# Causal attention block on one core: the triangle of the diagonal steps added on TensorE instead of selected on GpSimd

## The reference

```
xm = layernorm(x, g1, be1) * (1 + sc_a) + sh_a
q, k, v = split(xm @ Wqkv)
scores = q @ k.T * 32**-0.5
scores = where(tril, scores, -inf)          # causal: key <= query
x = x + gt_a * ((softmax(scores) @ v) @ Wproj + bproj)
xm = layernorm(x, g2, be2) * (1 + sc_m) + sh_m
x = x + gt_m * (gelu(xm @ W1 + b1) @ W2 + b2)
```

## Time and profile before

| | |
|---|---|
| median of three runs | 2166.22 us (2165.55 to 2166.54) |
| profiled execution, span | 2163.8 us |
| TensorE busy | 2126.4 us, 98% |
| VectorE busy | 1290.6 us, 60% |
| GpSimd busy | 958.5 us, 44% |
| ScalarE busy | 930.1 us, 43% |
| attention's score matmuls, first and last start | 332.2 and 1356.8 us |

### The profile page before, as it was taken

How to read it: one execution, slowest core, us unless ns; L and a number is a source line. 1 busy time by engine, 2 the same in 40 slices (tenths; PEclk the granted TensorE clock), 3 DMA queues, 4 the chain that set the end, 5 groups by cost and what they waited for, 6 DMA issues and landing times.

```text
span 2163.8 us, 30729 instructions
## 1 busy us (share of the span) xinstructions
PE 2126.4 (98%) x11326; PEld 1428.5 (66%) x11326; DVE 1290.6 (60%) x2872; ACT 930.1 (43%) x1780; POOL 958.5 (44%) x383
## 2 busy tenths in 40 slices
PE   8999999999999999999999999999999999999999
PEld 7888885444544445454544544778888888888887
DVE  5878877777777777777777756784312312122122
ACT  2111115566566666666666566435322222222221
POOL 2001007989799797988979784770000000000000
PEclk9999999999999999999999999999999999999999
DMA  7448347234361523625244324694201011011010
GB/s 287 180 156 265 134 168 186 49 89 107 70 143 47 122 55 76 142 65 132 51 95 94 70 70 135 202 326 156 97 1 59 15 44 59 1 59 59 1 39 20
DMA packets 129310, 223.29 MB, mean 103 GB/s; under 512 B 8574, under 2 KB 26054, under 8 KB 128968
## 3 DMA queue, kind: packets, MB, share of 16 engines
q1 hardware_dynamic: 108568, 180.43, 30.6%
q10 hardware_dynamic: 20592, 40.90, 5.0%
HBM read 146.31 MB, written 74.98 MB: 102 GB/s over the span
## 4 chain that ended last, share of the span: by engine, by line
PE 78%; POOL 11%; DVE 5%; issue 3%; DMA 2%; ACT 1%; SPq 0%; POOLq 0%; DVEq 0%; ACTq 0%; PEldq 0%
PE m_hid L1973 16%; PE p_acc L1987 16%; PE acc L861 12%; POOL psum_k L1208 10%; PE st L1453 9%; PE mx L1433 9%; PE o_ps L1470 9%; PE r_ps L1477 2%; DVE part L1313 2%; PE r_ps L1491 1%; PE p_acc L1952 1%; PE misc L815 1%; PE acc L839 1%; PE tp L825 1%; ACT prob L1252 1%
## 5 line engine op out<-in xcount | busy, mean ns | idle before, releaser
L1252 ACT ACTIVATE prob<-st 128x512 f32<-128x512 f32 (+3 forms) x1280 | 609.1, 540 | 374.3 <-PE st L1453 353.5
L1208 POOL TENSOR_TENSOR psum_k<-psum_k,prob 128x2048 f32<-128x2048 f32 (+1 forms) x150 | 663.9, 4426 | 20.7 <-ACT prob L1252 5.8
L1313 DVE TENSOR_REDUCE part<-mx 128x1 f32<-128x512 f32 x707 | 457.9, 685 | 75.0 <-PE mx L1433 70.6
L1453 PE MATMUL st<-q_st,k_st 98*128 98x512 f32 (+3 forms) x1280 | 491.0, 395 | 4.0 <-PE r_ps L1477 1.4
L1433 PE MATMUL mx<-k_st,qx_st 96*128 96x512 f32 (+3 forms) x1196 | 442.8, 395 | 10.3 <-DVE part L1313 2.8
L1453 PEld LDWEIGHTS st<-q_st,k_st 98*128 98x128 f32 x1280 | 241.3, 189 | 267.2 <-ACT prob L1252 152.3
L1874 DVE TENSOR_TENSOR m_g_lo<-m_g,m_g_hi 128x512 fp32r<-128x512 f32 x128 | 88.6, 692 | 479.7 <-ACT m_g_hi L1791 479.5
L1433 PEld LDWEIGHTS mx<-k_st,qx_st 96*128 96x128 f32 x1196 | 223.5, 189 | 129.9 <-DVE part L1313 60.4
L1470 PE MATMUL o_ps<-prob,v_sb 128*32 128x512 f32 (+3 forms) x2560 | 297.4, 539 | 3.7 <-POOL prob L1191 3.7
L1309 DVE CUSTOM_DVE_ANT_0 unused<-mx,mask_row 128x512 bf16<-128x512 f32 (+2 forms) x489 | 228.9, 486 | 119.0 <-PE mx L1433 109.0
L1784 ACT ACTIVATE m_g<-m_hid,vcol 128x512 f32<-128x512 f32 x128 | 88.3, 690 | 471.5 <-PE m_hid L1973 471.4
(11 more groups left out here) (186 smaller groups left out, 2529.2 us busy)
## 6 DMA issues: line engine op xcount, KB each, us to landing
k_st<-qk_scratch SPq DMA_DIRECT2D x96, 256.0 KB, 8.0
qx_st<-qk_scratch SPq DMA_DIRECT2D x96, 256.0 KB, 5.0
q_st<-qk_scratch SPq DMA_DIRECT2D x96, 256.0 KB
qk_scratch<-st_hi ACTq DMA_DIRECT2D x16, 1024.0 KB, 4.2
qk_scratch<-st_lo ACTq DMA_DIRECT2D x16, 1024.0 KB, 6.9
xs<-in_x_dram SPq DMA_DIRECT2D x8, 1024.0 KB, 8.9
v_sb<-v_scratch SPq DMA_DIRECT2D x8, 1024.0 KB, 15.6
o_scratch<-o_sb SPq DMA_DIRECT2D x32, 256.0 KB, 2.3
```

Source lines behind the costliest of these rows:

```text
L1208: nc.gpsimd.tensor_tensor(dst, src, prob[:, s % BUF, :, m:], ALU.add).then_inc(pool_added, 1)
L1252: nc.scalar.activation(prob[:, s % BUF, h, m:], st[n % RING][:, m:], ACT.Exp, scale=SCALE).then_inc(exp_done, 1)
L1313: nc.vector.tensor_reduce(most, bank[:, 0:w], AX.X, ALU.max).then_inc(mx_free, 1)
L1453: nc.tensor.matmul(st[n % RING][:, m:], k_st[u][0:MROWS, h, kt * P:(kt + 1) * P], q_st[0:MROWS, pos % 2, h, m:], start=True, stop=True).th ...
```

## The change

The constants get two more members, a bf16 identity `ident_bf` and `mask_col`, a 128 x 128 bf16 tile that holds 0 where key <= query and -1e30 elsewhere (keys on partitions). For each head of a diagonal step TensorE issues a second matmul behind the score matmul, with the identity as weights and `mask_col` as moving operand, into the leftmost 128 columns of the same bank and in the same accumulation group. The score then holds -1e30 in the triangle, and its exponential is zero. `select` and all waits on `b_masked` go, from GpSimd and from TensorE. The counts of the constants' semaphore go from 5 to 9 and from 6 to 10. No item of the plan moves; the planner's prices are as they were.

```diff
@@ constants, GpSimd, start of phase_qkv
-            pool.wait_ge(c_ready, 3)
+            nc.gpsimd.memset(K.ident_bf[:, :], 0.0).then_inc(c_ready, 1)
+            nc.gpsimd.memset(K.mask_col[:, :], 0.0).then_inc(c_ready, 1)
+            pool.wait_ge(c_ready, 5)
...
+            nc.gpsimd.affine_select(out=K.ident_bf[:, :], in_=K.ident_bf[:, :], compare_op=ALU.not_equal, fill=1.0, base=0,
+                                    pattern=[[-1, P]], channel_multiplier=1).then_inc(c_ready, 1)
+            nc.gpsimd.affine_select(out=K.mask_col[:, :], in_=K.mask_col[:, :], compare_op=ALU.is_ge, fill=NEG,
+                                    base=0, pattern=[[1, P]], channel_multiplier=-1).then_inc(c_ready, 1)
@@ TensorE, start
-            pe.wait_ge(c_ready, 5)
+            pe.wait_ge(c_ready, 9)
@@ GpSimd, attention
-            def select(g, s):
-                n, m = L.selects.index(s), L.mid(s)
-                await_count(pool, held_pool, exp_done, exp_count(g, GH * (s + 1)))
-                tri = prob[:, s % BUF, :, m:m + P]
-                nc.gpsimd.affine_select(out=tri, in_=tri, compare_op=ALU.is_ge, fill=0.0, base=0,
-                                        pattern=[[0, GH], [1, P]], channel_multiplier=-1).then_inc(masked, 1)
@@ add, GpSimd
-                if L.diagonal(s):
-                    pool.wait_ge(masked, mask_count(g, L.selects.index(s) + 1))
@@ body, GpSimd
-                    if s in L.selects:
-                        select(g, s)
@@ scores, TensorE
-                    nc.tensor.matmul(st[n % RING][:, m:], k_st[u][0:MROWS, h, kt * P:(kt + 1) * P],
-                                     q_st[0:MROWS, pos % 2, h, m:], start=True, stop=True).then_inc(st_ready, 1)
+                    ins = nc.tensor.matmul(st[n % RING][:, m:], k_st[u][0:MROWS, h, kt * P:(kt + 1) * P],
+                                           q_st[0:MROWS, pos % 2, h, m:], start=True, stop=not L.diagonal(s))
+                    if L.diagonal(s):
+                        ins = nc.tensor.matmul(st[n % RING][:, m:m + P], K.ident_bf[:, :], K.mask_col[:, :], start=False, stop=True)
+                    ins.then_inc(st_ready, 1)
@@ product, TensorE
-                if L.diagonal(s):
-                    pe.wait_ge(masked, mask_count(g, L.selects.index(s) + 1))
```

More of the change, by code:

```diff
@@ L73, in __init__ @@
         self.ones = sb("ones", [P, P])
+        self.ident_bf = sb("ident_bf", [P, P], BF16)
+        self.mask_col = sb("mask_col", [P, P], BF16)
         self.vcol = sb("vcol", [P, V_ROWS])
@@ L207, in __init__ @@
         self.NA = self.sums[True].NA
-        self.selects = [s for s in range(self.NS) if self.diagonal(s)]
-        self.ND = len(self.selects)
         FROM = -3
@@ L969, in phase_attention @@
         exp_done = sem("b_exp_done")
-        masked = sem("b_masked")
         pv_done = sem("b_pv_done")
@@ L990, in phase_attention @@
         held_dve = sem("b_dve_wait_carrier")
-        held_pool = sem("b_pool_wait_carrier")
         def st_count(g, tiles):
@@ L1005, in add_count @@
             return L.NA * g + n + L.NA
-        def mask_count(g, n):
-            return L.ND * g + n
         def item_count(g, n):
@@ L1181, in key_ones @@
             def key_ones(h):
-                pool.wait_ge(masked, mask_count(0, sum(r <= ONES + h for r in L.selects)))
                 pool.wait_ge(pool_added, add_count(0, L.NA))
@@ L1549, in tensor @@
             pe.sem_inc(r_ready, 2)
-            pe.wait_ge(E.c_ready, 6)
+            pe.wait_ge(E.c_ready, 10)
             pe.wait_ge(E.mx_free, len(L.opening))
```

## The result

The changed kernel takes 2184.8 us (median of 4 runs, 2183.7 to 2185.9), the kernel before 2166.2 in the same session: ratio 1.0085, interval 1.0073 to 1.0097, so 18.7 us slower. The forecast was 2200, with a range of 2176 to 2240. Direction and range were right, the size was not: +34 forecast, +18.7 found.

A forecast was written before the change was run, and what follows sets the result against it. The prediction took TensorE to bound the kernel. To the runs' median of 2166.22 us it added 38 us for the masks and took off 4 us for the waits: 2200 us, with a range of 2176 to 2240.

The forecast's parts named there:

- TensorE bounds: Attention stage: TensorE, busy 127.1 of a head group's 129.0 us, is the limit; a group grows to 133 to 134.
- The selects: GpSimd's 128 selects, 82 us of its work, are worth TensorE's waits on the path: gain 4 us, at most 16.
- The raw price: Diagonal steps: 512 mask matmuls at 0.11 us each, whatever the width of their scores product, 56 us.
- E: Rival: masks on TensorE cost their stream alone, 0.06 us each; +17 us, 2183; chance 0.09.
- The hidden share: Diagonal steps: stalls let a third of the masks' added time vanish, leaving 38 of 56 us.
- The end of a chunk: Query chunk's end: the last diagonal step's select runs behind an add, and its product starts after 0.31 us of idling.
- A: Rival: masks hidden nowhere, +52 us, 2218; chance 0.21 with what lies about it, to 2235.
- B: Rival: the change of type shows both weight loads, 0.28 us per mask; +103 us, 2269; chance 0.09.
- D: Rival: no measurable change, stalls swallow nearly all masks and regained waits pay the rest; 2166; chance 0.04.
- C: Rival: GpSimd is the hidden pacemaker of the head groups, so the change is faster; -16 us, 2150; chance 0.07.
- The small edits: Start moves by up to 1 us, covered by the Wada wait; semaphores and adds shift slightly: cost 0, without slack 1.

The follow-up runs named there:

- neither: Changed kernel without its masks, so neither selects nor masks and the causal triangle left in: 2161.62 us, ratio 0.9979 to the kernel before.
- narrow: Changed kernel with the mask product 32 columns wide in place of 128: 2185.10 us, ratio 1.0086 to the kernel before.
- both: Kernel before with the masks added on TensorE and GpSimd's selects kept: 2185.87 us, ratio 1.0088.
- light kernels: VectorE's plain maximum reads 128 of 512 columns; with neither selects nor masks 2118.70 us, with masks in place of selects 2154.52 us.
- double: Changed kernel with each mask product issued twice in a row: 2208.19 us, ratio 1.0191 to the kernel before.
- light kernel with selects: Kernel before with VectorE's plain maximum reading a quarter of its columns: 2155.31 us, ratio 0.9944.
- changed light kernel: Changed kernel with VectorE's plain maximum reading a quarter of its columns: 2154.52 us, ratio 0.9945 to the kernel before.
- swap later: Kernel before with a chunk's last diagonal select ahead of the preceding add, in groups behind the first only: 2164.83 us, ratio 0.9992.

## Why the prediction was right in direction and too large

**TensorE bounds, the group shows it: right.** The chain goes through TensorE for 94%. The group grew by the masks: 129.0 to 131.3 us, where 133 to 134 was forecast. Diagonal steps grew by 0.06 to 0.45 us, under the 0.6 that would have refuted the price.

**The selects: right alone, wrong in the sum.** Forecast 4 us, from TensorE's waits; measured 4.65 (neither against before). But with the masks in, the selects would have cost only about 1 us. The two terms are not additive: the masks had given the selects their time already.

**The raw price: right in mechanism, a little high.** 0.11 for each mask, because of the fp32r load behind it, was seen in the timeline, and narrow confirmed it. I had written "whatever the width of its scores product", and that failed: behind a 128-wide score it is 0.07, since there, too, a load is the limit without a mask, and the identity's load is half as long. 53 us in place of 56. The sign that I had named for it misled: the maximum starts 0.04 us behind the mask, which by "0.06 after the mask's start means E" would speak for E. The delay shows at the next score (0.32 us behind the maximum's start, 0.24 before), so the price has to be read from score to score. The 81 ns of the Trainium skill ("TensorE: Matmul & The Clock Gate", back-to-back issue gap) for a matmul of 128 columns would give 41 us; the first mask's price behind a wide score doesn't agree with it, while the second mask's 0.07 lies between that section's two figures. The halved load that the Trainium skill states for 128 non-FP32 columns (same title, weight-path perf modes) is seen in the rows, 97 ns for bf16 against 189 for fp32r; it bears on the second mask and on masks behind a 128-wide score.

**The hidden share: the step that failed.** "I let a third of the added time vanish: 56 x 2/3 = 38 us." Of 53 us, 23.2 show (after against neither) or 19.6 (both against before): 56 to 63% vanish. I had seen the stalls, put them at 0.3 us a step, and then argued that part of them were late weight loads which stay. The waits view had a number that I did not use: 99.6 us of loads of maxima held by VectorE. A mask stands just ahead of such a load, on the same engine, so time that the load would have waited passes with the mask. The light kernels show it: with the holds of plain maxima gone, 5.7 of 6.6 us per group show, in place of 3.0, so 2.7 x 8 = 21 us were hidden there. The count of holds itself is no measure of that. It fell by 37.7 us (99.6 to 61.9), but the mask's own load now stands in part of that idle time (50.3 us put down to "issue" at L1445), and under the second mask, of which 8 to 13 us do not show, it fell by 1.8 more (to 60.1). ScalarE's holds of score banks rose from 152.3 to 159.3.

**The end of a chunk: half seen.** Behind the masks, three blocks of two steps at chunk ends got shorter, by 0.54 (the select's wait), 0.18 and 0.02 us in the group. The diagonal steps grew by 3.07 in all, and 3.07 - 0.74 = 2.3 is the group's growth. The 0.18 is there with the selects or without (neither 6.28, after 6.09, double 5.91 us): presumably a later TensorE finds VectorE and ScalarE ahead when the chunk ends, so that part of what showed at the steps is given back there; no run tests it.

**The rivals.** A (nothing hidden) fell with the hidden share. B (both loads exposed at the change of type) fell in the timeline: from score to score a mask adds 0.07 to 0.13 us, nothing like 0.28. D (all swallowed) fell by the result. E by narrow. C (GpSimd as hidden pacemaker) was not the case, but was nearer than I gave it: as soon as VectorE is light, GpSimd's selects cost 36.6 us, the lower clock behind the waits for them included.

**The small edits: right.** The longer start is covered by the wait for Wada, 1.1 us shorter; ScalarE's waits for adds went from 12.4 to 9.1 us, and no run set them apart from the rest; GpSimd is busy 882.8 us, where 877 was forecast.

## What to carry to other kernels

When work is added to the engine that bounds, look up its own waits just behind the place of insertion: a hold by another engine there can take up the added work. The waits view shows where and not how much: here 99.6 us of holds hid some 21 of 53 us of masks. Price a short matmul by the weight load that has to follow it, not by its columns. And when two variants come out equal, make the two that complete the square (neither, and each alone): 36 us against 36 looked like nothing here.

## What the runs showed of the hardware

**A short matmul's price.** 32 and 128 columns of bf16 between fp32r matmuls cost the same, 0.11 to 0.12 us behind scores of 256 columns and more and 0.07 behind 128; a second one with the same operands 0.06 to 0.07. The change between bf16 and fp32r inside one accumulation group showed no price of its own.

**The clock behind waits of one or two microseconds.** The kernel before shows none of this in its attention stage. In the light kernel with selects TensorE waits for GpSimd for 2.83 us in its first group, 1.96 at the start of its second (for the key-row memsets) and 1.97 in its third, and each time the clock falls to 1.2 GHz. Sixteen more waits for a select in the same execution, of 1.1 to 1.7 us, have no drop behind them. The windows view of the third, as of 640 us (granted clock third from the end):

```profile
640.00:644.00 4.00, 4.00 (x18) 2.19 (x17) 1.74 (x7) 1.11 (x4) 4.00 (x2) 0.52 0.29 73
644.00:648.00 4.00, 4.00 (x11) 3.23 (x11) 1.72 (x6) 2.67 (x5) 4.00 (x3) 0.50 0.63 128
648.00:652.00 4.00, 4.00 (x26) 2.15 (x28) 1.28 (x4) 2.11 (x4) 1.40 (x2) 0.50 0.02 8
652.00:656.00 4.00, 4.00 (x35) 2.04 (x23) 1.58 (x5) 1.77 (x4) 3.43 (x1) 0.77 0.00 0
```

That is 1.97 us of waiting and then 4 x (0.48 + 0.50 + 0.50 + 0.23) = 6.8 us of full-clock work lost, before what other engines' idle time takes up; 13.6 us at the three places together. The group that holds it lasts 130.5 us from first score to first score, the four behind it 126.3. It is part of the 36.6 us that selects cost there. The changed light kernel has no such drop in its attention stage. Waits of 0.83, 1.00 and 0.85 us left the clock as it was in the kernel before, but one of 0.80 us in "swap later" had the drop behind it. So a wait of TensorE can cost several times its length, its length alone doesn't tell whether it will, and it isn't so in every execution.
